# A fused attention and mixture-of-experts layer: lighter routing bookkeeping, and the attention gate folded into the projection weights

## The reference: what is computed

```
h = layernorm(x) * (1 + ca) + sa
x = x + ga * (attention(h) @ Wo)      # 16 heads of 16; 4 sink keys and a window of the last 128
h = layernorm(x) * (1 + cb) + sb
x = x + gb * moe(h)
```

```
shared = (silu(x @ ws_gate) * (x @ ws_up)) @ ws_down
scores = sigmoid(x @ gate_w.T);  top 2, normalised to sum 1, times 2.5
routed = sum over the two experts of weight * (silu(x @ w_gate[e]) * (x @ w_up[e])) @ w_down[e]
```

## Time and profile before

| | us |
|---|---|
| three runs | 348.56, 348.93, 351.56 |
| median | 348.93 |
| the profiled execution, first to last instruction | 347.5 |
| busy: PE, DVE, POOL, ACT | 278.8, 231.3, 205.2, 162.2 |
| mean granted TensorE clock, as a share of 2.4 GHz | 0.913 |

### The profile page before, as it was taken

The page is one execution under the profiler, slowest core; times in us unless marked ns, Lnnn a source line. Parts: engine busy times, 40 slices in busy tenths (PEclk is TensorE's granted clock), DMA queues, the critical chain, the costliest instruction groups (busy, mean ns, idle before and its releaser), DMA issues.

```text
span 347.5 us, 6287 instructions
## 1 busy us (share of the span) xinstructions
PE 278.8 (80%) x1665; PEld 215.0 (62%) x1666; DVE 231.3 (67%) x899; ACT 162.2 (47%) x518; POOL 205.2 (59%) x254
## 2 busy tenths in 40 slices
PE   4897889998988899989774999898899898886000
PEld 3264457656766576757543989787788787775000
DVE  0477477998889886997885645544345477763990
ACT  3142562278225822556222455454545566654550
POOL 3713116738784777558557356564655578875981
PEclk9996996999899996999988799999999999999555
DMA  7949001133624649702286644454456778869793
GB/s 261 330 132 347 16 2 49 59 100 115 197 80 135 183 127 320 163 30 93 72 228 205 201 138 121 144 177 133 138 160 180 245 210 254 263 188 343 247 360 139
DMA packets 41438, 59.80 MB, mean 172 GB/s; under 512 B 5092, under 2 KB 29880, under 8 KB 41404
## 3 DMA queue, kind: packets, MB, share of 16 engines
q1 hardware_dynamic: 34312, 39.91, 39.4%
q0 software_dynamic: 6528, 17.90, 14.3%
q10 hardware_dynamic: 564, 1.59, 1.4%
HBM read 33.57 MB, written 25.80 MB: 171 GB/s over the span
## 4 chain that ended last, share of the span: by engine, by line
PE 54%; DVE 22%; DMA 7%; issue 7%; ACT 4%; POOL 2%; another core or an unknown queue 1%; SPq 1%; DVEq 0%; POOLq 0%; ACTq 0%
PE bank L1227 16%; PE bank L892 8%; PE bank L1237 8%; PE bank L1085 6%; PE bank L1029 3%; PE bank L1052 3%; DVE bank L1752 3%; PE bank L1105 3%; DMA ht<-in_L_attn_x_dram 2%; PE bank L1067 2%; DVE h_sb L1369 2%; DMA ys<-pt_win,row_i 2%; PE bank L935 1%; PE bank L906 1%; DMA p_win<-slots 1%
## 5 line engine op out<-in xcount | busy, mean ns | idle before, releaser
L648 POOL DMA_INDIRECT ys<-pt_win,row_i x72 | 72.6, 1009 | 51.0 <-ACT pt_win L676 27.5
L1227 PE MATMUL bank<-ht,w_now 128*128 128x128 f32 x576 | 78.3, 280 | 4.4 <-issue 4.4
L593 POOL DMA_INDIRECT slots<-h_sb,slot_i x64 | 63.2, 987 | 30.1 <-issue 15.3
L1227 PEld LDWEIGHTS bank<-ht,w_now 128*128 128x128 f32 x576 | 71.7, 195 | 5.4 <-issue 5.1
L1741 DVE TENSOR_TENSOR act_t<-bank,sg 128x128 f32<-128x128 f32 x72 | 20.9, 290 | 48.5 <-ACT sg L843 33.2
L676 ACT ACTIVATE ht<-bank 128x256 f32<-128x256 f32 x104 | 39.9, 383 | 22.5 <-PE bank L892 15.6
L1237 PE MATMUL bank<-w_dn,act_t 128*128 x144 | 44.8, 393 | 5.4 <-DVE act_t L1741 4.3
L676 ACT ACTIVATE pt_win<-bank 128x256 f32<-128x256 f32 (+1 forms) x88 | 37.2, 423 | 21.7 <-PE bank L1237 9.6
L1085 PE MATMUL bank<-w_route,ht 128*128 128x272 f32 x128 | 41.5, 452 | 5.5 <-ACT ht L676 3.2
L892 PE MATMUL bank<-ident,p_win 128*128 128x128 f32 x198 | 36.1, 278 | 4.9 <-issue 3.2
L843 ACT ACTIVATE sg<-bank 128x128 f32<-128x128 f32 x72 | 20.1, 279 | 42.2 <-PE bank L1227 29.6
(11 more groups left out here) (260 smaller groups left out, 489.2 us busy)
## 6 DMA issues: line engine op xcount, KB each, us to landing
p_win<-slots SPq DMA_DIRECT2D x67, 129.0 KB
slots<-pads SPq DMA_DIRECT2D x28, 129.0 KB
xs<-in_L_attn_x_dram SPq DMA_DIRECT2D x3, 1024.0 KB
wmod_sb<-ys SPq DMA_DIRECT2D x12, 256.0 KB
w_gu<-ys SPq DMA_DIRECT2D x10, 256.0 KB, 2.8
mod_bc<-mod_rows_out SPq DMA_DIRECT2D x4, 512.0 KB, 5.7
w_dn<-in_L_ffn_w_down_dram SPq DMA_DIRECT2D x1, 2048.0 KB
h_sb<-ys SPq DMA_DIRECT2D x8, 256.0 KB
```

The costliest lines, as they stand in the source:

```text
L593: pool.indirect_dma_start(out=slots, out_offset=bass.IndirectOffsetOnAxis(ap=slot_i[:, k, j:j + 1], axis=0), in_=h_sb[:, j, :], in_offset= ...
L648: pool.indirect_dma_start(out=ys, out_offset=bass.IndirectOffsetOnAxis(ap=row_i[:, col:col + 1], axis=0), in_=y_sb[:, k, :], in_offset=Non ...
L1227: last = mm(bank[2 + k % 2][:, half * P:(half + 1) * P], w_now[:, k % 2, c, half * M:(half + 1) * M], ht[:, k, c, :], start=(c == 0), stop ...
```

## The change

1. `chosen` keeps only the comparison: it reads `top_i` (unsigned integers) directly and writes `hot_b` in bf16, one mask for each choice. The cast, the sum of masks, the two copies into the rows' spare columns, the copy of the scores and the running count go. `top_v` and `top_i` are kept for all 32 tiles, so the scores are read from `top_v` later.
2. The two copies into the spare columns move to ACT (`row_cols`), two instructions for each part; POOL's `scatter` waits for both them and the row numbers.
3. `rank` sums both masks on PE: two products with the triangle, two for each earlier tile, and a fifth block of columns, "the tile after the last", whose ranks are the running first rows. They start from `base_rows`, in fp32, brought in by a product with the fp32 identity. DVE copies the fifth block to `base_rows` for the next half.
4. `ranked` multiplies `hot_b` with the ranks straight from PSUM; `placed` sums directly into the integers. The adding of the experts' first rows and the last cast go.
5. `early_table` and `expert_table` take counts out of `base_rows` (a subtraction more each); the product of counts on PE (`cnt_ps`) goes.
6. POOL multiplies Wo with the attention's gate once a batch (`wo_gated`, 128 x 512), right after `wsd_gated`; `at_project` uses it and waits for it, and `at_add` is one addition.
7. `sm_x1` gets memory of its own instead of a part of `o_g`; one memset in the setup goes.

```diff
+            def gated_projection(b):
+                pool.wait_ge(S["ld_wv"], 32)
+                if b > 0:
+                    pool.wait_ge(S["at_out"], b)
+                pool.tensor_tensor(wo_gated[:], wo_sb[:], mbc(b, GA).unsqueeze(1).to_broadcast([P, C, D]), ALU.mult)\
+                    .then_inc(S["wo_ready"], 1)
+
+            def placed_rows(part):
+                pool.wait_ge(S["cols_ready"], 2 * part)
+                pool.wait_ge(S["slots_ready"], part)
...
                 pool.tensor_tensor(wsd_gated[:], wsd_sb[:], mbc(b, GB), ALU.mult).then_inc(S["wsd_ready"], 1)
+                gated_projection(b)
                 if b > 0:
                     scatter(GROUP + 2)
...
+            def row_cols(half, lo=0, hi=GROUP):
+                b, g = divmod(half, GPB)
+                first = half * GROUP + lo
+                r = slice(g * GROUP + lo, g * GROUP + hi)
+                act.wait_ge(S["top_ch"], 2 * (half * GROUP + hi))
+                copy(h_sb[:, r, D], token2[:, ds(first, hi - lo)]).then_inc(S["cols_ready"], 1)
+                copy(h_sb[:, r, D + 1], top_i[:, first:first + hi - lo, 0]).then_inc(S["cols_ready"], 1)
...
                 else:
+                    row_cols(b * GPB - 1)
                     second_keys(b, range(3, CH))
...
                 h_copy(b, 4)
+                row_cols(b * GPB)
...
                 pe.wait_ge(S["at_ots"], b + 1)
+                pe.wait_ge(S["wo_ready"], b + 1)
                 for k in range(C):
-                    last = mm(bank[5][:, 0:D], o_t[:, k, :], wo_sb[:, k, :], start=(k == 0), stop=(k == C - 1))
+                    last = mm(bank[5][:, 0:D], o_t[:, k, :], wo_gated[:, k, :], start=(k == 0), stop=(k == C - 1))
...
-                mm(o, ones_b[:], counted_b[:, half, :].unsqueeze(1).to_broadcast([P, hi - lo, NE]), start=True,
-                   stop=False, skip_group_check=True)
-                mm(o, before_b[:], mask_b[:, lo:hi, :].rearrange("p t e -> p (t e)"), start=False, stop=False,
-                   skip_group_check=True)
-                for i in range(hi - 1):
+                top = hi + (hi == GROUP)
+                mm(blocks(lo, top), ident[:], base_rows[:, half:half + 1, :].to_broadcast([P, top - lo, NE]),
+                   start=True, stop=False, skip_group_check=True)
+                for k in range(TOPK):
+                    mm(blocks(lo, hi), before_b[:], hot_b[:, k, lo:hi, :].rearrange("p t e -> p (t e)"), start=False,
+                       stop=False, skip_group_check=True)
+                for i in range(top - 1):
                     to = max(i + 1, lo)
-                    last = mm(bank[3][:, D + to * NE:D + hi * NE], ones_b[:],
-                              mask_b[:, i:i + 1, :].to_broadcast([P, hi - to, NE]), start=False,
-                              stop=(i == hi - 2), skip_group_check=True)
+                    for k in range(TOPK):
+                        last = mm(blocks(to, top), ones_b[:], hot_b[:, k, i:i + 1, :].to_broadcast([P, top - to, NE]),
+                                  start=False, stop=(i == top - 2 and k == TOPK - 1), skip_group_check=True)
...
-                at.done(v.tensor_tensor(o_g[:], bank[5][:, 0:D], mbc(b, GA), ALU.mult))
                 tail = xcols(b * TPB + TPB - 1)
-                v.tensor_tensor(tail, tail, o_g[:], ALU.add).then_inc(S["at_x"], 1)
+                v.tensor_tensor(tail, tail, bank[5][:, 0:D], ALU.add).then_inc(S["at_x"], 1)
...
-                rt.done(v.tensor_copy(top_if[:, lo:hi, :], top_i[:, r, 0:TOPK]))
-                rt.done(v.tensor_tensor(hot[:, :, lo:hi, :],
...
-                v.tensor_tensor(mask_b[:, lo:hi, :], hot[:, 0, lo:hi, :], hot[:, 1, lo:hi, :], ALU.add)\
-                    .then_inc(S["masks"], 1)
-                for col, src in ((D, token2[:, ds(first, n)]), (D + 1, top_if[:, lo:hi, 0])):
...
-                v.tensor_copy(val_all[:, :, ds(first, n)], top_v[:, r, 0:TOPK].rearrange("p t k -> p k t"))\
...
-                    rt.done(v.tensor_reduce(mask_sum[:], mask_b[:].rearrange("p t e -> p e t"), AX.X, ALU.add))
-                    rt.done(v.tensor_tensor(counted_b[:, half + 1, :], counted_b[:, half, :], mask_sum[:], ALU.add))
+                v.tensor_tensor(hot_b[:, :, lo:hi, :],
+                                expert_no[:].unsqueeze(1).unsqueeze(1).to_broadcast([P, TOPK, n, NE]),
+                                top_i[:, first:first + n, 0:TOPK].rearrange("p t k -> p k t").unsqueeze(3)
+                                .to_broadcast([P, TOPK, n, NE]), ALU.is_equal).then_inc(S["masks"], 1)
...
-                v.tensor_tensor(place[:, lo:hi, :], bank[3][:, D + lo * NE:D + hi * NE].rearrange("p (t e) -> p t e", e=NE),
-                                expert_row[:].unsqueeze(1).to_broadcast([P, n, NE]), ALU.add)\
+                if hi == GROUP:
+                    v.tensor_copy(base_rows[:, half + 1, :], bank[3][:, D + GROUP * NE:D + (GROUP + 1) * NE])\
...
+                v.tensor_tensor(at_place[:, :, lo:hi, :],
+                                bank[3][:, D + lo * NE:D + hi * NE].rearrange("p (t e) -> p t e", e=NE).unsqueeze(1)
+                                .to_broadcast([P, TOPK, n, NE]), hot_b[:, :, lo:hi, :], ALU.mult)\
                     .then_inc(S["rank_read"], 1)
...
-                rt.done(v.tensor_tensor(at_place[:, :, lo:hi, :],
-                                        place[:, lo:hi, :].unsqueeze(1).to_broadcast([P, TOPK, n, NE]),
-                                        hot[:, :, lo:hi, :], ALU.mult))
-                rt.done(v.tensor_reduce(slot_f[:, :, lo:hi], at_place[:, :, lo:hi, :], AX.X, ALU.add))
-                v.tensor_copy(slot_i[:, :, g * GROUP + lo:g * GROUP + hi], slot_f[:, :, lo:hi])\
+                    v.tensor_reduce(slot_i[:, :, g * GROUP + lo:g * GROUP + hi], at_place[:, :, lo:hi, :], AX.X, ALU.add)\
...
+                    tb.done(v.tensor_tensor(full_c, base_rows[:, FULL_BY + 1, :], expert_row, ALU.subtract))
+                    tb.done(v.tensor_scalar(full_c, full_c, 1.0 / P, -(P - 1) / (2.0 * P), ALU.mult, ALU.add))
```

More of the change, by code:

```diff
@@ L575, in _ @@
                              allow_small_or_imprecise_dtypes=True))
-            c.done(pool.iota(expert_row[:], pattern=[[CAP * P, NE]], base=0, channel_multiplier=0,
+            c.done(pool.iota(expert_row, pattern=[[CAP * P, NE]], base=0, channel_multiplier=0,
                              allow_small_or_imprecise_dtypes=True))
@@ L642, in _ @@
             for part in range(HALVES - 1, PARTS):
-                pool.wait_ge(S["slots_ready"], part + 1)
+                placed_rows(part + 1)
                 for i in range(PART):
@@ L825, in _ @@
                 h_copy(b, 7)
+            row_cols(HALVES - 1, 0, PART)
             tanh(B, 0)
             act_copy(B, 0)
+            row_cols(HALVES - 1, PART, GROUP)
             act_copy(B, 1)
@@ L853, in _ @@
             act.wait_ge(S["tables"], 1)
-            act.activation(e_neg[:], val_all[:].rearrange("p k t -> p (k t)"), ACT.Exp, scale=-1.0)\
+            act.activation(e_neg[:].rearrange("p (k t) -> p k t", k=TOPK),
+                           top_v[:, :, 0:TOPK].rearrange("p t k -> p k t"), ACT.Exp, scale=-1.0)\
                 .then_inc(S["e_ready"], 1)
```

84 lines of the change are left out of this document (29 added, 55 removed).

## The result

The changed kernel took 353.77 us (median of 6 runs, 352.63 to 357.13), beside 349.66 us for the kernel before: a ratio of 1.0105, 95% interval 1.0067 to 1.0143. Measured again later it was 350.96 us beside 347.11, 1.0149 (1.0084 to 1.0214). So it is 1.0 to 1.5% slower, 3.7 to 5.2 us. The forecast was 349.1 us and no change, with a range of 344.0 to 353.5 us; 353.77 us lies 0.3 us above its upper end. But the forecast was added up on 348.93 us for the kernel before, which measured 349.66 here: carried over to that base, the two ratios give 352.6 and 354.1 us, the first inside the range, the second above it.

The account below looks back on a forecast made before the run. No single limit in the batch stage: PE and DVE both nearly full, waiting for each other. Terms +0.2 + 0 + 0 = +0.2 us; 347.5 + 0.2 + 1.4 = 349.1 us, range 344.0 to 353.5.

Parts of the forecast that it names:

- the sentence that the forecast rested on: Batch stage: DVE gets rid of some 12 us of work and the time stays, as relief falls where DVE waits for PE.
- The first rival: Batch stage: DVE's relief counts nearly everywhere, 7.0 us less 8 x 0.31 on PE: -4.5, so 344.4 us; chance 0.18.
- Batch 3's wait for the maxima: Batch 3's first half: ACT's 0.88 us wait for DVE's maxima goes, less PE's 0.31: -0.57 us.
- POOL's lateness: Scatters to next tiles' `h_tile`: POOL's 1.47 us multiplication lies whole on the chain in three batches, +4.4, 353.5 us; chance 0.14.
- What of this is on the path: Batch stage, three kinds of place: middles +0.2 us, first halves about 0, middle of batch 3 to expert stage 0.
- its term for `rank`: PE's rank, full halves: ten bf16 products and one fp32 at 0.18 us add 0.31 us each, bounds 0 and 0.62.
- PE's wait of 0.66 us: Batch 1's middle: PE waits for the attention's normalised output, which comes 0.2 us earlier, so 0.2 us is gained.
- the last two parts: End of the batch stage: they stand behind ACT's tanh and the early tiles' landing, so they cost 0.
- 0, where PE waits anyway: Lower bound for a full rank's growth on PE, beside the 0.31 us taken and 0.62 at half clock.
- a loss in one batch alone: Sign in the batch stage: time lost or won in one batch only points to clock or entry, not routing.
- DVE's tile behind POOL's longer multiplication: Batch stage, `h_tile`: waits for POOL's multiplication, nothing takes it in; three batches at 0.65 us, +2.0, 351.1 us; chance 0.08.
- the fourth rival: Entry to the expert stage: the 3.85 us wait goes away under a different instruction sequence, 345.2 us; chance 0.08.

Follow-up runs that it names:

- idle products in the rank: Kernel before, routing whole, plus unread products on PE in each rank (one fp32 of 80 columns, five bf16 in full ranks): 355.11 us, ratio 1.0166.
- the routing alone: Changed kernel with the output gate's multiplication back on DVE and no multiplication of the projection's weights on POOL: 356.12 us, ratio 1.0205.
- the gate alone: Kernel before with only the output gate folded into the projection's weights on POOL, its routing untouched: 352.97 us, ratio 1.0064.
- the short rank: Changed kernel with counts and mask sum back on DVE, first rows from a bf16 table, no fp32 product in the rank: 353.08 us, ratio 0.9956.

## Why the prediction was right or wrong, point by point

**What held.** DVE's relief shows no gain: the sentence that the forecast rested on. DVE's busy time fell by 9.6 us (12 forecast), its wait in the middle grew to 1.66 us (1.5 or more), and the pair of kernels with 220.0 and 230.7 us of DVE work took the same time within their intervals. The other busy times were further off: PE +5.3 us (2 to 3 forecast), POOL +3.9 (6; its new multiplication takes 1.27 us, not 1.47), ACT +2.5 (4). The first rival, that the relief counts nearly everywhere, falls with that. Batch 3's wait for the maxima went: from the start of `tanh` to the exponentials it was 150.65 - 147.28 = 3.37 us and is 152.94 - 150.23 = 2.71, a gain of 0.66 (0.57 forecast). In batch 1 the same stretch grew from 76.23 - 73.69 = 2.54 us to 76.69 - 73.97 = 2.72, by 0.18 (0.31 forecast).

That the range takes in the first measurement, by its ratio, is luck. Its upper end, 353.5 us, stands for POOL's lateness, which the runs refute as the cause. My own bounds, with rank anywhere between 0 and 0.62 us, ended at 351.6.

**The step that failed** is the one called "What of this is on the path", in its term for `rank`. It has two faults.

First the size. I took 0.18 us for the fp32 product from two products of 32 columns. With 80 columns it takes 0.18 in the first halves too (75.50 to 75.68 us in batch 1), but 0.26 to 0.27 in the middles. So a rank in a middle grows by 0.40 us, not 0.31 (in a first half by 0.31, as forecast), and by more where it falls into a half-clock stretch: 0.86 us long in batch 2's middle with idle products, 0.81 in batch 1's in the second profile of after. This adds some 0.4 us at full clock. It is the smaller fault.

Second the netting. I set the rank's growth against DVE's shorter tail in the middles, against PE's wait of 0.66 us, and against batch 3's wait of 0.88 us, and came to +0.2. The runs show no such relief: 3.5 us more on PE in the rank (2.8 in full halves, 0.7 in the last parts) cost 4.2 to 7.4 us with DVE's work unchanged, 1.6 us in the middles alone 1.6 to 5.5, some 2.9 us of which most stood in PE's recorded waits 2.6 to 5.8, and 2.8 us less on PE gave 0.4 to 3.9. A price of 1.2 to 1.4 us of time for one of PE fits all four; the routing alone, 7.2 us (5.4 to 8.9) with 2.5 in full halves, cost more than that. With 2.5 us in full halves at one for one, my own sum would have been 347.5 + 2.5 + 1.4 = 351.4 us; on the same base it measured 352.6 and 354.1.

One of the waits was misread as well. The 0.66 us of the earlier trace rows is idle time of the weight load (PEld), and I gave it to PE. PE's own products run on right up to it, and in batch 0, for which I wrote that PE has no wait there, the same row has 0.72 us. Batch 0, then batch 1:

```profile
56.88 0.29 PEld L892 LDWEIGHTS bank<-ident,o_n 128*128 128x128 f32 x2 [0.72 <-DVE o_n L1330]
```

```profile
91.96 1.84 PE L1085 MATMUL bank<-w_route,ht 128*128 128x272 f32 x4
93.68 0.69 PE L892 MATMUL bank<-ident,o_n 128*128 128x128 f32 x2
```

A smaller term was put at nothing and isn't quite: "the last two parts". Ahead of the last of them DVE now waits 1.73 and 3.37 us for PE. From batch 3's tile 7 to the last row numbers it is 8.59 us before, and 8.76 and 10.82 in the two profiles after. No run prices it by itself.

The bound "0, where PE waits anyway" was the wrong lower end: it took PE's recorded waits at their word, although PE's records may begin before a wait has ended, as I had noted ahead of the forecast. The Trainium skill, "Perfetto Trace Analysis", section "Tensor Engine Instruction (MATMUL, LD_WEIGHTS)", says that the end of a matrix product in a trace is computed from its size and not observed, and that the semaphore goes out only when PSUM has acknowledged the data. The 0.03 to 1.20 us between the end of PE's records and ACT's copy agree with that, in that the record doesn't say when the result is there.

**What a trace of mine would have misled to.** I had written that a loss in one batch alone would point to the clock or the entry. The first profile shows its largest piece, 2.9 us, at the entry, and the runs with the long rank speak against it: the routing alone and the idle products in the rank are as slow as this kernel, or slower, at the same mean clock as the kernel before. The half-clock stretches move from profile to profile. The wait at the entry, 3.85 us before, is 6.17 us in one profile of after and 4.16 in the other; but it is 4.58 to 6.80 us in the six other kernels whose rank is old or short, 6.80 with the gate alone. The 3.85 us are the shortest of all 14 profiles, so a comparison with that one trace may make the entry look dearer than it is.

**The other rivals.** POOL: both its signs are in the profile (the cover gone, 0.18 us, and new waits of 0.39 us for a scaled tile ahead of `h_tile` for tile 5), yet without its multiplication the kernel is no faster. The signs were right and the price wrong; why the delayed pieces cost so little was not traced. DVE's tile behind POOL's longer multiplication: in batch 1 `h_tile` for tile 4 starts at 85.70 us, takes 0.70 us in place of 0.48, and ends 0.29 us after the multiplication (84.84 + 1.27 = 86.11): 0.22 us, not 0.65. The rule that the Trainium skill gives for the pair of ports ("SBUF — State Buffer", section "SBUF: two separate sides"), that the later one waits for the whole of the earlier, would have put the end at 86.59; it was 86.40. L1436, which I had said agrees with that rule, ended 0.15 us after its multiplication and not the 0.29 it takes alone: both are held up, neither for the whole, as far as POOL's spans can tell, which are rough in a profile. The wait at the entry (the fourth rival; the forecast's sum of chances calls it the third) did not go away.

**What stays open.** Why a microsecond more on PE seems to cost more than one: a half-clock stretch makes some of it longer (the rank took 0.86 us in one, 0.53 outside), and the time between PE's records and its consumers differs from batch to batch, but no run here separates the two. Why the routing alone costs more than the idle products of its size, although DVE has less to do. And the sign of the gate's fold.

## What to carry to other kernels

Where PE and another engine are both nearly full, price PE's additions at one for one at least, wherever they stand, and don't net them against gaps in PE's own records; look at when its consumers get their data. Moving work from DVE to PE as "free" small products is a trade, and an fp32 product of 80 columns costs as much as seven to ten small bf16 ones. When a difference is near 1%, a twin with idle work of the same size tells what two traces can't.

## What the hardware showed that was not expected

An fp32 product of 80 columns takes 0.18 us on PE in the first halves and 0.26 to 0.27 in the middles, one of 32 columns 0.18, while a small bf16 product takes 0.026 to 0.027: seven to ten for one. The sum of two bf16 masks on DVE takes 0.19 us by itself in the short rank's profile. In batch 1's middle it took 0.60 us (87.78 to 88.38 us), beside a POOL multiplication from 87.50 to 88.33 us, and again 0.60 in batch 3's middle beside another.
